# Low parts on VectorE, squares and roots moved, and short transposes merged, in a two-layer transformer kernel on one core

## The reference, cut to what matters

```python
h = jnp.einsum('nf,ibf->nib', xf, W1b)
h = jax.nn.gelu(h, approximate=False) * mask[:, :, None]
y = jnp.einsum('nib,fib->nf', h, W2b)
```

```python
attn = jax.nn.softmax(scores, axis=-1)
out = jnp.einsum('bhqk,bhkd->bhqd', attn, v)
...
h = silu(x @ gate.T) * (x @ up.T)
y = h @ down.T
out = x + y / sqrt(mean(y * y) + 1e-6)
```

## Time and profile before

| | us |
|---|---|
| median of 3 runs | 2230.88 (2230.74 to 2238.21) |
| the profiled execution | 2236.44 |
| its span | 2234.7 |
| PE busy | 2069.3, 93% |
| DVE busy | 1536.4, 69% |
| ACT busy | 844.8, 38% |
| POOL busy | 441.3, 20% |

### The profile page before, as it was taken

One profiled execution on the slowest core, in us unless ns is written; L12 is line 12 of the kernel. 1 busy time (PEld: TensorE's weight loads), 2 busy tenths in 40 slices (PEclk: granted clock), 3 DMA queues, 4 the chain that ended last, 5 costly groups with the idle time before them and its releaser, 6 DMA issues. The chain is left out here.

```text
span 2234.7 us, 52900 instructions
## 1 busy us (share of the span) xinstructions
PE 2069.3 (93%) x21680; PEld 1461.3 (65%) x21680; DVE 1536.4 (69%) x2407; ACT 844.8 (38%) x1773; POOL 441.3 (20%) x280
## 2 busy tenths in 40 slices
PE   7999979999997999979899998999988899999997
PEld 5777758887786788724444544445445688787776
DVE  6544333798976355589999999999995330577776
ACT  4322122222223200055655665555653322244443
POOL 0111112223220154400110010100101444211111
PEclk9999989999998999969999999999999899999999
DMA  5122244344327633424444454444543655320101
GB/s 185 58 96 77 76 150 170 104 135 135 126 77 283 184 113 128 141 81 121 127 121 125 119 143 128 120 123 116 142 124 102 226 172 177 104 76 27 49 1 38
DMA packets 209147, 268.18 MB, mean 120 GB/s; under 512 B 42336, under 2 KB 123552, under 8 KB 206240
## 3 DMA queue, kind: packets, MB, share of 16 engines
q1 hardware_dynamic: 208064, 264.85, 38.3%
q10 hardware_dynamic: 864, 0.21, 0.0%
HBM read 181.81 MB, written 83.17 MB: 119 GB/s over the span
## 5 line engine op out<-in xcount | busy, mean ns | idle before, releaser
L1688 ACT ACTIVATE a_prob<-ps,a_nmax 128x256 f32<-128x256 f32 (+7 forms) x512 | 377.1, 739 | 311.9 <-DVE a_nmax L1727 214.5
L1797 PE MATMUL ps<-xacc 64*128 64x512 f32 (+5 forms) x1536 | 382.5, 540 | 69.5 <-ACT a_prob L1688 63.2
L1727 DVE TENSOR_REDUCE a_nmax<-ps 128x1 f32<-128x1024 f32 (+3 forms) x256 | 256.3, 1001 | 31.3 <-PE ps L1797 30.9
L1797 PEld LDWEIGHTS ps<-xacc 64*128 64x128 f32 x1536 | 144.1, 194 | 187.2 <-ACT a_prob L1688 127.8
L1748 DVE STREAM_TRANSPOSE a_pt_long<-a_prob 128x768 f32<-128x768 f32 (+1 forms) x256 | 237.8, 929 | 0.0
L2111 DVE SCALAR_TENSOR_TENSOR f_part<-ps,f_gu_scale,f_part 128x512 f32<-128x512 f32 x264 | 184.9, 746 | 66.7 <-PE ps L2158 53.4
L1812 PE MATMUL ps<-a_pt_long,xacc 32*64 32x256 f32 (+1 forms) x6144 | 206.7, 377 | 6.0 <-issue 3.9
L1716 POOL TENSOR_TENSOR a_o<-a_o,a_rd 128x1024 f32<-128x1024 f32 x31 | 73.0, 2356 | 696.3 <-ACT a_o L1698 686.3
L1812 PEld LDWEIGHTS ps<-a_pt_long,xacc 32*64 32x64 f32 x6144 | 121.0, 133 | 107.8 <-issue 98.3
L945 POOL TENSOR_TENSOR f_hT_lo<-f_h,f_hT_hi 128x512 fp32r<-128x512 f32 x64 | 94.2, 1480 | 276.6 <-ACT f_hT_hi L928 276.6
L1794 PE MATMUL ps<-xacc 64*128 64x128 bf16 x1024 | 112.5, 225 | 6.1 <-ACT a_prob L1688 6.0
(11 more groups left out here) (234 smaller groups left out, 4463.1 us busy)
## 6 DMA issues: line engine op xcount, KB each, us to landing
xacc<-scratch_QT SPq DMA_DIRECT2D x512, 64.0 KB, 2.1
scratch_QT<-k_qo SPq DMA_DIRECT2D x64, 256.0 KB, 2.3
xacc<-scratch_V SPq DMA_DIRECT2D x64, 256.0 KB, 4.8
a_rd<-scratch_R SPq DMA_DIRECT2D x64, 256.0 KB, 4.4
scratch_OT<-a_o SPq DMA_DIRECT2D x32, 512.0 KB, 3.9
o_of<-scratch_OT SPq DMA_DIRECT2D x30, 512.0 KB, 4.0
f_block<-in_packed SPq DMA_DIRECT2D x33, 256.0 KB, 3.4
xacc<-in_x SPq DMA_DIRECT2D x8, 1024.0 KB, 6.4
```

The costliest lines, as they stand in the source:

```text
L1688: last = nc.scalar.activation(prob[:, n % PRING, s].rearrange("p (a w) -> p a w", w=w), SC[n % 2][:, a, 0:w], ACT.Exp, bias=nmax[:, n % 4, ...
L1727: nc.vector.tensor_reduce(nmax[:, n % 4, 0:1], SC[n % 2][:, :, 0:width(0, t)], AX.XY, ALU.max, negate=True).then_inc(maxed, 1)
L1797: last = pe.matmul(sc[:, a, 0:w], q[r, slot, heads[a * hf], :], kt[r, b, keys], start=not masked, stop=True, skip_group_check=True)
```

## The change

In feed_forward0 DVE makes the low parts of the blocks 0 to 2, each right after the next block's product; POOL keeps the one of block 3, with a semaphore of its own (h_last). Four of the unpack steps move ahead of the weight pair. The load of the shift column is counted on scale_in. In attention1 the two heads of a short tile are turned by one instruction with one more dimension, and LONG_VALUES moves one block later by a step at four places. In feed_forward1 the squares stand ahead of step 2's silu, the root ahead of step 3's; DVE updates two tiles in step 4 and two in step 5. For the last chunk the copies are left out: ACT loads the root's table early with a small root, squares each tile out of PSUM as it is done, and takes its root; DVE updates tile by tile out of PSUM. POOL's low part of feed_forward1 stays.

```diff
@@ feed_forward0: gpsimd
-                        it = c + q * NCH
-                        for b in range(BPQ):
-                            pool.wait_ge(h_hi.sem, h_hi.now(it, b + 1))
-                            nc.gpsimd.tensor_tensor(hT[1][:, b, :], h[:, b % 2, :], hT[0][:, b, :].bitcast(F32),
-                                                    ALU.subtract).then_inc(h_lo.sem, 1)
+                        b = BPQ - 1
+                        pool.wait_ge(h_hi.sem, h_hi.now(c + q * NCH, b + 1))
+                        nc.gpsimd.tensor_tensor(hT[1][:, b, :], h[:, b % 2, :], hT[0][:, b, :].bitcast(F32),
+                                                ALU.subtract).then_inc(h_last.sem, 1)
@@ feed_forward0: vector
+                            if b:
+                                dve.wait_ge(h_hi.sem, h_hi.now(it, b))
+                                nc.vector.tensor_tensor(hT[1][:, b - 1, :], h[:, (b - 1) % 2, :],
+                                                        hT[0][:, b - 1, :].bitcast(F32), ALU.subtract
+                                                        ).then_inc(h_lo.sem, 1)
                             if b < BPQ - 1:
                                 unpack_some(range(2 * b, 2 * b + 2))
+                        unpack_some(range(2 * BPQ - 2, 2 * BPQ + 2))
                         if q + 1 < NQ:
                             split((q + 1) % 2, c, c + (KC + q * NCH))
...
-                        unpack_some(range(2 * BPQ - 2, OPS))
+                        unpack_some(range(2 * BPQ + 2, OPS))
@@ attention1
-               40: range(11, 13), 41: range(13, 15), 42: range(15, 18), 43: range(18, 21), 44: range(21, 24),
-               45: range(24, 28), 46: range(28, 32)}
+               40: range(11, 13), 41: range(13, 15), 42: range(15, 17), 43: range(17, 20), 44: range(20, 23),
+               45: range(23, 27), 46: range(27, 32)}
...
+                    if hf:
+                        src = prob[:, n % PRING, 0:2 * blocks * 32].rearrange("p (h j k) -> p h j k", h=2, k=32)
+                        last = nc.vector.transpose(
+                            pt_short[:, 0:blocks, heads[0]:heads[0] + 2, t, :].rearrange("p j h q -> p h j q"), src)
@@ feed_forward1: scalar
+                def squares(c):
+                    act.wait_ge(y_out, TPC * (c + 1))
+                    for t in range(TPC):
+                        nc.scalar.activation(square[:], y[:, t, :], ACT.Square, accum_out=ss[:, t:t + 1]
+                                             ).then_inc(rooted, 1)
+                        act.wait_ge(rooted, (TPC + 1) * c + t + 1)
+                def root(c):
+                    if c:
+                        act.wait_ge(ready, (TPC + 1) * (c - 1) + 1)
+                    nc.scalar.activation(rms[:], ss[:], ACT.Sqrt, bias=eps[:], scale=1.0 / C).then_inc(rooted, 1)
+                    act.wait_ge(rooted, (TPC + 1) * (c + 1))
+                def last_roots():
+                    act.wait_ge(ready, LAST)
+                    nc.scalar.activation(square[:, 0:1], eps[:], ACT.Sqrt).then_inc(rooted, 1)
+                    for t in range(TPC):
+                        act.wait_ge(y_done, TPC * (NF - 1) + t + 1)
+                        act.wait_ge(rooted, LAST + 2 * t + 1)
+                        nc.scalar.activation(square[:], YB[t], ACT.Square, accum_out=ss[:, t:t + 1]
+                                             ).then_inc(rooted, 1)
+                        act.wait_ge(rooted, LAST + 2 * t + 2)
+                        nc.scalar.activation(rms[:, t:t + 1], ss[:, t:t + 1], ACT.Sqrt, bias=eps[:], scale=1.0 / C
+                                             ).then_inc(rooted, 1)
...
-                        gate(s)
+                        if c and n == 2:
+                            squares(c - 1)
                         if c and n == 3:
                             root(c - 1)
-                for t in range(TPC):
-                    copy_y(NCH - 1, t)
-                root(NCH - 1)
+                        gate(s)
+                last_roots()
@@ feed_forward1: vector
                     if c and n == 4:
-                        finish(c - 1)
-                finish(NCH - 1)
+                        invert(c - 1)
+                        finish(c - 1, (0, 1))
+                    if c and n == 5:
+                        finish(c - 1, (2, 3))
+                finish_last()
```

More of the change, by code:

```diff
@@ L880, in _ @@
                 chunk(NCH - 1, False)
[L881 removed]
+                sp.dma_start(up_shift[:], d["c_up_shift"]).then_inc(scale_in.sem, 16)
                 for p in range(PARTS):
@@ L971, in unpack @@
                     elif i == 6:
-                        dve.wait_ge(scale_in.sem, scale_in.now(m, 16))
+                        dve.wait_ge(scale_in.sem, scale_in.now(m, 2 * 16))
                     if i == 0:
@@ L1002, in _ @@
                     if q == 1:
-                        dve.wait_ge(shift_in.sem, 16)
+                        dve.wait_ge(scale_in.sem, 2 * 16)
                     unpacking = q and (q, c0, c1) != SEGMENTS[-1]
@@ L1061, in _ @@
                                     pe.matmul(YB[t], part, w2[s][:, p, b, :], start=b == 0 and s == 0, stop=False)
-                            pe.wait_ge(h_lo.sem, h_lo.now(it, b + 1))
+                            if b < BPQ - 1:
+                                pe.wait_ge(h_lo.sem, h_lo.now(it, b + 1))
+                            else:
+                                pe.wait_ge(h_last.sem, h_last.now(it, 1))
                             for t in range(TPC):
@@ L1740, in turn @@
                     blocks = 4 * (t + 1)
-                    for i, h in enumerate(heads):
-                        src = prob[:, n % PRING, i * blocks * 32:(i + 1) * blocks * 32]
-                        src = src.rearrange("p (j k) -> p j k", k=32)
-                        if hf:
-                            last = nc.vector.transpose(pt_short[:, 0:blocks, h, t, :], src)
-                        else:
-                            near = min(blocks, MAIN)
-                            last = nc.vector.transpose(pt_long[:, unit % 2, 0:near, h, t - 4, :], src[:, 0:near, :])
-                            if blocks > MAIN:
-                                last = nc.vector.transpose(pt_wide[:, unit % 2, 0:blocks - MAIN, h, t - 6, :],
-                                                           src[:, MAIN:blocks, :])
+                    if hf:
+                        src = prob[:, n % PRING, 0:2 * blocks * 32].rearrange("p (h j k) -> p h j k", h=2, k=32)
+                        last = nc.vector.transpose(
+                            pt_short[:, 0:blocks, heads[0]:heads[0] + 2, t, :].rearrange("p j h q -> p h j q"), src)
+                    else:
+                        h = heads[0]
+                        src = prob[:, n % PRING, 0:blocks * 32].rearrange("p (j k) -> p j k", k=32)
+                        near = min(blocks, MAIN)
+                        last = nc.vector.transpose(pt_long[:, unit % 2, 0:near, h, t - 4, :], src[:, 0:near, :])
+                        if blocks > MAIN:
+                            last = nc.vector.transpose(pt_wide[:, unit % 2, 0:blocks - MAIN, h, t - 6, :],
+                                                       src[:, MAIN:blocks, :])
                     last.then_inc(turned, 1)
@@ L1997, in feed_forward1 @@
         PB = [ps[:, b * BANK:(b + 1) * BANK] for b in (4, 5, 6, 7)]
+        LAST = (TPC + 1) * (NCH - 1)
         widened = sem("widened")
@@ L2032, in _ @@
                     for t in range(c * TPC, (c + 1) * TPC):
-                        sp.wait_ge(ready, t + c + 2)
+                        i = t - c * TPC
+                        sp.wait_ge(ready, LAST + 2 * i + 2 if c == NCH - 1 else (TPC + 1) * c + i + 2)
                         sp.dma_start(d["out"][t * P:(t + 1) * P, :], xacc[:, t, :]).then_inc(stored, 16)
@@ L2063, in copy_y @@
                     nc.scalar.activation(y[:, t, :], YB[t], ACT.Copy).then_inc(y_out, 1)
-                def root(c):
+                def squares(c):
                     act.wait_ge(y_out, TPC * (c + 1))
```

18 lines of the change are left out of this document (13 added, 5 removed).

## The result

| | us | runs |
|---|---|---|
| before | 2231.93 (2230.74 to 2238.21) | 4 |
| after | 2206.12 (2196.99 to 2208.01) | 4 |
| ratio | 0.9872, 95% 0.9849 to 0.9895 | |
| predicted | 2203.2 (2196 to 2215) | |

The change is 25.8 us faster. A second comparison gave 2206.1 (2198.78 to 2210.69, 5 runs) against 2234.39 (11 runs), ratio 0.9862 (0.9842 to 0.9883). The profiled execution took 2207.36 us, its span is 2205.6.

The account below looks back on a forecast made before the run. PE bounds both feed-forwards, though DVE paces the first from 523 us; in the attention both are nearly full. Terms 4.6 + 4.5 + 13.4 + 5.2 = 27.7 us, taken from 2230.9, give 2203.2 us, range 2196 to 2215.

Parts of the forecast that it names:

- First feed-forward: First feed-forward: DVE's chunk falls from 22.93 to 20.35 us, below PE's 21.6; PE's pauses go, gaining 4.6 us.
- left-over collision: First feed-forward: POOL's one remaining low part still delays DVE's third unpack step, taken as 0.4 us (ends 0 and 1.0).
- Attention: Second attention: a score's wait of 0.24 us goes in 16 units, plus 0.7 us from transposes; gain 4.5 us.
- The 0.7 us for the last two transposes of a unit: Second attention: a gain of 0.7 us from merged transposes said to fall outside PE's full stretch.
- the third rival: Second attention: a merged transpose costs as much as its pair and PE keeps its waits; 2208 us, chance 0.06.
- Chunk ends: Second feed-forward: the pauses at three chunk ends vanish, gaining all 13.4 us (ends 7 and 14).
- the late table load: Second feed-forward chunk ends: the load back to silu's table makes step 3's silu 1.28 us late, PE's stall taken as 0.
- the updates in line: Second feed-forward chunk ends: two updates take 1.9 us, leaving DVE 0.8 us late, less than PE's half step.
- the second rival: Listed: DVE still bounds the first feed-forward, 2213 us, chance 0.10; the label also went to a 2.66 us table switch.
- the first: Rival, second feed-forward: held table load or inline updates keep a 2 us pause per chunk end; 2209 us, chance 0.17.
- The end: Kernel's end after PE's last matmul: early table load and tile-by-tile squares, roots and updates gain 5.2 us (4 to 6).
- the fourth: Rival, second attention: the merged transpose runs at half rate, making the kernel slower, about 2277 us; chance 0.03.

Follow-up runs that it names:

- unpack_back: Changed kernel with the four unpack steps behind the weight pair again: 2200.25 us in one execution, then 2208.75 us over five rounds, ratio 0.9893.
- values_only: Kernel before with the changed table of long values (LONG_VALUES) alone: 2229.02 us against 2233.73.
- merge_only: Kernel before with the merged transposes alone and the old table of long values: 2229.48 us against 2233.73.
- held_both: Changed kernel with the root's table load also held behind the last addition, making step 3's silu later: 2207.43 us.
- four_updates: Changed kernel with all four residual updates of the second feed-forward's chunk ends in step 4: 2208.98 us.
- ff0_only: Kernel before with the changed first feed-forward alone: 2233.84 us against 2233.73.
- load_early: Changed kernel with the wait for the root behind step 3's silu, so silu's table load no longer stands behind a wait: 2206.8 us.

## Why the prediction was right, and where it was not

**The sum** was right for the reason given: 27.7 us predicted, 27.9 in the stretches, and each stretch within 1 us of its term. That the profiled execution came within 1.3 us of the predicted 2208.7 (2207.36) is in part luck: its attention as a whole gained 1.7 us, less than half of the predicted 4.5, and 3.4 us came from two stretches that the change leaves alone, the one between the first feed-forward and the attention's first maximum (284.4 us before, 283.1 after) and the one from the last maximum to the second feed-forward's first silu (221.9 and 219.9). The predicted median of 2203.2 is 2.9 too low, inside the runs' own spread (2196.99 to 2208.01): 1.05 of it is the median before, which a fourth run moved from 2230.88 to 2231.93, and the other 1.9 that the medians differ by 25.8 us and not by 27.7. In the second comparison they differ by 28.3.

**First feed-forward**, 4.6 predicted, 4.9 measured. Right: four pauses gone, the bound back to PE, whose chunk is 21.75 us (21.6 in the prediction). Mis-sized: DVE's chunk, 20.35 predicted and 20.8 measured. The left-over collision was taken as 0.4 us on the third unpack step; it is 0.92 us on the second (L975). I had reasoned that the subtraction ahead of the steps leaves less of POOL's instruction to meet them. It only moves the steps back by one place: POOL still has 1.1 us to go when the next one begins (503.50 + 1.42 - 503.80, as 642.14 + 1.32 - 642.35 in the earlier trace rows), and the price is what the earlier trace rows already showed. The Trainium skill ("SBUF — State Buffer", section "Who interferes with whom") would have said that this step can be blocked too: it lists DVE's tensor_scalar with the operations that can enter the modes that take the port pair shared with GpSimd, and says that the other side is then blocked whole. 1.41 us beside 0.49 agree. Not needed was the removal of the 1.37 us wait by the moved unpack steps: unpack_back has a wait of 0.77 us there and the same length.

**Attention**, 4.5 predicted, 3.6 measured on undisturbed units. The 0.24 us a unit is right, with the wait that was named, and it comes from the moved value blocks alone (values_only), not from the transposes. The 0.7 us for the last two transposes of a unit was wrong: I had argued that they lie outside PE's full stretch, and did not follow who waits there. What waits is PE, for ScalarE's exponents, for a maximum that DVE makes before these transposes (merge_only). The merged transposes' 7.7 us of DVE (114.1 to 106.4 us, 105.0 predicted) thus bring nothing in an undisturbed unit. In this half the third rival had the outcome right, but not its reason: a merged transpose is cheaper than its pair.

**Chunk ends**, 13.4 predicted, 14.35 measured. The pauses are gone, and the two doubtful steps, the late table load and the updates in line, are hidden as argued. In this stretch of the kernel before, 35 of PE's 840 matmuls start 0.32 to 2.56 us behind the one ahead of them, in the changed kernel none over 0.3 us. What these 35 take over the pace of 0.23 us is 13.9 us: 8.4 us of waits, and 5.5 us of slower matmuls. Some 3 us of the latter lie behind two of the six waits, where the granted clock fell to 0.50 (1.2 GHz, the lower level). A window of the kernel before, behind a wait of 2.16 us that ended at 2095.78:

```profile
2098.00:2100.00 2.00, 2.00 (x6) 1.61 (x5) 1.38 (x3) 0.27 (x2) 0.19 (x1) 0.50 0.00 0
```

The table load took 1.28 us with no drain behind it: loads start at 2000.93 and 2004.83, and what follows them at 2002.22 and 2006.12. The 2.66 us that the Trainium skill ("ScalarE: Activation LUTs", section "What ACT_TABLE_LOAD costs") gives for a switch of tables are seen in no row. held_both, 2.9 us late, tells that a silu as late as that would have kept some of the gain away; the prediction calls this the second rival, but it belongs to the first. The pair of updates takes 1.4 us and not 1.9: half of 3.77 was the wrong price, because the group of four contains one that POOL's low part blocks (in four_updates POOL runs from 2010.90 to 2012.29, inside the 3.78 us): four times 0.71 and 0.94 on top.

**The end**, 5.2 predicted, 5.1 measured, by the steps given: a tile takes 1.11 us where 1.05 was taken, an update 0.75 where 0.69 was.

**Rivals.** The first (a pause stays at chunk ends), the second (DVE stays the bound) and the fourth (half rate) fell.

## What to carry to other kernels

Of a stall, price the whole pause, not the wait row alone: three chunk ends showed 8.4 us of waits and cost 14. To find whether shorter work on a full engine helps, follow the wait that ends last there: work behind the instruction that is waited for is worth nothing, and moving a few other blocks was worth 0.24 us a unit for free. When parts of 4 us are tested, compare stretches between two fixed instructions in one profile each, since totals scatter more than that; then say of the total only what several runs show.

## What the runs showed of the hardware that I had not expected

**A fall of the clock that comes and goes.** Units of attention with the same code take 46.17 us or 47.59 us. Windows of the kernel before, a unit of 47.59 us, and the same place in a unit of 46.17 us:

```profile
1159.00:1161.00 2.00, 0.99 (x6) 0.38 (x6) 2.00 (x4) 1.18 (x3) 0.00 (x0) 1.00 0.40 115
1161.00:1163.00 2.00, 1.52 (x14) 0.56 (x22) 2.00 (x4) 2.00 (x5) 0.52 (x1) 0.73 0.00 0
1163.00:1165.00 2.00, 2.00 (x36) 0.93 (x35) 2.00 (x4) 1.07 (x3) 1.84 (x1) 0.50 0.04 8
...
1254.00:1256.00 2.00, 0.99 (x6) 0.38 (x6) 2.00 (x4) 1.18 (x3) 0.00 (x0) 1.00 0.44 124
1256.00:1258.00 2.00, 1.27 (x15) 0.68 (x23) 2.00 (x4) 2.00 (x5) 0.34 (x1) 1.00 0.07 20
1258.00:1260.00 2.00, 2.00 (x51) 1.03 (x43) 2.00 (x4) 1.07 (x3) 2.00 (x1) 1.00 0.04 8
```

The granted clock is 0.50 (1.2 GHz, the lower level) for some 3 us in the one and 1.00 in the other, although PE was busy for the same 0.99 of 2 us before; the unit is 1.42 us longer. Which units are hit differs between executions: in the changed kernel's first profile the ninth unit to be compared took 46.53 us and the tenth and eleventh 45.93 and 46.14, in its second 45.93, 47.31 and 47.55. Over 15 units these disturbances add 10.4 us in the profile of before (702.9 against 15 x 46.17) and 12.1 in that of after (701.1 against 15 x 45.93), which hides half of the 3.6 us gained there. In the other profiles they range from 4.8 us (merge_only) to 15.7 (ff0_only), both with the old table. So whether the change makes them rarer or more frequent can't be told. What decides whether the clock falls at such a place was not tried, and not every long unit was traced to it.

**GpSimd's grip on a short DVE instruction.** L975, 0.49 us alone, took 1.41 beside POOL's subtraction, and that one 1.42 instead of 1.29 (POOL at 2008.50 in the changed kernel): the collision costs DVE 0.92 us here.

**A table load behind waits.** ScalarE stood idle for 2.30 us before a load of 1.28 us that needs no result of another engine: in the kernel before, the same load ran at 2021.34, right behind the instruction ahead of it, while its silu waited until 2023.75. Taking one wait away from in front of it (load_early) left the time as it was, since the load's delay was hidden.
